# One exp over two PSUM banks in place of two, in the attention phase of a transformer layer on 8 cores

## The reference

```python
x = x + _layernorm(attn(_layernorm(x)))    # x: [4, 4096, 2048]
x = x + _layernorm(ffn(_layernorm(x)))
...
scores = jnp.einsum('bhqd,bhkd->bhqk', q, k) * scale      # 32 half-heads of 64
scores = jnp.where(causal, scores, jnp.finfo(scores.dtype).min)
probs = jax.nn.softmax(scores, axis=-1)
attn_out = jnp.einsum('bhqk,bhkd->bhqd', probs, v)
attn = attn_out[:, 0::2] - lambda_full * attn_out[:, 1::2]
attn = attn * jax.lax.rsqrt(jnp.mean(attn * attn, axis=-1, keepdims=True) + EPS) * ln_w
```

## Time and profile before

| | us |
|---|---|
| median of 3 runs | 10618.79 |
| lowest and highest of them | 10558.02, 11322.63 |
| the profiled execution, its time | 10558.02 |
| its span on the slowest core (core 4) | 10556.5 |
| spans of the 8 cores | 10413.7 to 10556.5 |
| TensorE matmul busy | 8300.7 (79%) |
| ScalarE busy | 3346.5 (32%) |
| VectorE busy | 2612.8 (25%) |

### The profile page before, as it was taken

The page is one execution under the profiler, slowest core; times in us unless marked ns, Lnnn a source line. Parts: engine busy times, 40 slices in busy tenths (PEclk is TensorE's granted clock), DMA queues, the critical chain, the costliest instruction groups (busy, mean ns, idle before and its releaser), DMA issues. The chain is left out here.

```text
span 10556.5 us, 119745 instructions; the slowest of 8 cores (10413.7 to 10556.5 us)
## 1 busy us (share of the span) xinstructions
PE 8300.7 (79%) x43898; PEld 4033.8 (38%) x44754; DVE 2612.8 (25%) x4091; ACT 3346.5 (32%) x4745; POOL 396.6 (4%) x385
## 2 busy tenths in 40 slices
PE   3456456666767774999999999991999999999994
PEld 1233233334434442344444444441344444444442
DVE  2321454433332333111111111115111111111103
ACT  1223455656757773111111112113111111111112
POOL 0000000000000000000000000000000000000000
PEclk8778788888889987999999999995999999998896
DMA  4222301010000003554554554543554554444443
GB/s 105 79 65 72 59 7 39 9 37 4 8 30 10 4 6 97 80 73 67 80 74 66 79 75 66 79 56 127 80 73 67 80 73 66 69 70 75 58 62 80
DMA packets 642913, 635.29 MB, mean 60 GB/s; under 512 B 31247, under 2 KB 619280, under 8 KB 623410
## 3 DMA queue, kind: packets, MB, share of 16 engines
q0 software_dynamic: 569136, 436.44, 28.6%
q1 hardware_dynamic: 73218, 191.14, 5.5%
HBM read 1013.51 MB, written 50.36 MB: 101 GB/s over the span
## 5 line engine op out<-in xcount | busy, mean ns | idle before, releaser
L1248 PE MATMUL p3b_yps<-p3b_hg,p3b_w2c 128*128 128x512 bf16 x12416 | 2846.3, 390 | 167.4 <-DVE p3b_hg L1200 124.2
L1248 PEld LDWEIGHTS p3b_yps<-p3b_hg,p3b_w2c 128*128 128x128 bf16 x12672 | 1253.0, 100 | 1756.5 <-issue 437.8
L617 ACT ACTIVATE p_p<-p_s 128x512 bf16<-128x512 f32 x2816 | 1531.2, 595 | 387.4 <-PE p_s L592 208.1
L1161 PE MATMUL p3b_hps<-p_xfm,p3b_w1A 128*128 128x512 bf16 x6774 | 1526.6, 386 | 52.9 <-DMA p3b_w1A<-rw 45.1
L592 PE MATMUL p_s<-p_q,p_k 128*128 128x512 bf16 x2543 | 969.7, 409 | 668.1 <-ACT p_p L617 416.9
L1161 PE MATMUL p3b_hps<-p_xfm,p3b_w1B 128*128 128x512 bf16 x5642 | 1268.7, 385 | 6.6
L1277 DVE TENSOR_TENSOR p_acc<-p3b_yps,p_acc 128x1024 f32<-128x1024 f32 x544 | 666.2, 1225 | 2434.8 <-PE p3b_yps L1248 2400.4
L1189 ACT ACT_TABLE_LOAD x396 | 508.1, 1283 | 2239.0 <-PE p3b_hps L1161 2221.0
L1161 PEld LDWEIGHTS p3b_hps<-p_xfm,p3b_w1A 128*128 128x128 bf16 x6912 | 681.4, 99 | 896.4 <-issue 172.4
L565 PE MATMUL p_pv<-p_v,p_p 128*128 128x129 bf16 x5632 | 845.6, 230 | 198.7 <-DVE p_p L633 197.4
L633 DVE TENSOR_TENSOR p_p<-p_p,p_mask 128x512 bf16<-128x512 bf16 x1536 | 652.7, 425 | 1395.1 <-ACT p_p L617 1219.7
(11 more groups left out here) (153 smaller groups left out, 3367.2 us busy)
## 6 DMA issues: line engine op xcount, KB each, us to landing
p3b_w2c<-rw POOLq DMA_DIRECT2D x256, 704.0 KB, 7.7
p3b_w1A<-rw POOLq DMA_DIRECT2D x32, 3072.0 KB, 19.2
p3b_w1B<-rw POOLq DMA_DIRECT2D x32, 2560.0 KB, 19.5
p_xt<-xseq SPq DMA_DIRECT2D x32, 1024.0 KB, 12.7
p3a_xm<-xmid_scr SPq DMA_DIRECT2D x32, 1024.0 KB, 8.5
p3b_w2c<-sw POOLq DMA_DIRECT2D x32, 704.0 KB, 7.4
p_xt<-xown SPq DMA_DIRECT2D x16, 1024.0 KB, 11.4
p_xo<-xown SPq DMA_DIRECT2D x16, 1024.0 KB, 6.9
```

Of the source, the lines that this page charges most:

```text
L617: tok = C.inc(eng.activation(out=dst[:], in_=s3_ps[:, bank * 512:(bank + 1) * 512], func=AF.Exp, scale=0.125), "S")
L1161: ins = eng.matmul(out=h_ps[hp][:, ts_ * 512:(ts_ + 1) * 512], lhsT=wbuf[:, dc * width + fcl * 128:dc * width + (fcl + 1) * 128], rhs=xfm2 ...
L1248: ins = eng.matmul(out=y2_ps[cb][:, ts_ * 512:(ts_ + 1) * 512], lhsT=w2c[cw][:, fc * 256 + dcl * 128:fc * 256 + (dcl + 1) * 128], rhs=hg[: ...
```

## The change

The two exps of a slot become one instruction of 1024 elements that reads both banks of `s3_ps`. The four `pbuf` tiles of 512 columns become two of 1024, one for even and one for odd slots, the first map in columns 0 to 511 and the second in 512 to 1023. The counts on ScalarE's semaphore are halved with it. ScalarE waits for the second score matmul of a slot; the first score matmul of slot `s` waits for the whole exp of slot `s - 1`, the second has no wait of its own. In masked slots ScalarE waits for both halves of the mask of slot `s - 2`. VectorE still masks in two instructions of 512, but both come after the whole exp. All matmuls, masks and sizes of the work are otherwise the same.

```diff
-    pbuf = [s2(f"p2_p{i}", [P, 512], BF16) for i in range(4)]
+    pbuf = [s2(f"p2_p{i}", [P, 1024], BF16) for i in range(2)]
...
-                            C.wait(eng, "S", base_S + 2 * s + 2)
-                        p1 = pbuf[s % 2]
-                        p2 = pbuf[2 + s % 2]
+                            C.wait(eng, "S", base_S + s + 1)
+                        pq = pbuf[s % 2]
...
-                                             lhsT=p1[:, tt * 128:(tt + 1) * 128],
+                                             lhsT=pq[:, tt * 128:(tt + 1) * 128],
...
-                                             lhsT=p2[:, tt * 128:(tt + 1) * 128],
+                                             lhsT=pq[:, 512 + tt * 128:512 + (tt + 1) * 128],
...
-                            if k_idx >= 2:
-                                C.wait(eng, "S", base_S + k_idx - 1)
-                            else:
-                                C.wait(eng, "S", sb_prev[bank])
+                            if half == 0:
+                                C.wait(eng, "S", base_S + s if s >= 1 else sb_prev)
...
-                for _k in range(2 * Eg - 2, 2 * Eg):
-                    sbank_last[_k % 2] = base_S + _k + 1
+                sbank_last = base_S + Eg
...
-                        for half in range(2):
-                            k_idx = 2 * s + half
-                            bank = k_idx % 2
-                            C.wait(eng, "T", tok_mm[(s, half)])
-                            if s - 2 >= nm0:
-                                C.wait(eng, "V", base_V + 2 * (s - 2 - nm0) + 1 + half)
-                            dst = (pbuf[s % 2] if half == 0 else pbuf[2 + s % 2])
-                            tok = C.inc(eng.activation(
-                                out=dst[:], in_=s3_ps[:, bank * 512:(bank + 1) * 512],
-                                func=AF.Exp, scale=0.125), "S")
-                            assert tok == base_S + k_idx + 1
+                        C.wait(eng, "T", tok_mm[(s, 1)])
+                        if s - 2 >= nm0:
+                            C.wait(eng, "V", base_V + 2 * (s - 2 - nm0) + 2)
+                        tok = C.inc(eng.activation(
+                            out=pbuf[s % 2][:], in_=s3_ps[:, 0:1024],
+                            func=AF.Exp, scale=0.125), "S")
+                        assert tok == base_S + s + 1
...
-                            C.wait(eng, "S", base_S + 2 * s + 1 + half)
-                            if s - 2 >= 0:
-                                C.wait(eng, "T", tok_pv.get(s - 2, 0))
-                            src = pbuf[s % 2] if half == 0 else pbuf[2 + s % 2]
+                            if half == 0:
+                                C.wait(eng, "S", base_S + s + 1)
+                                if s - 2 >= 0:
+                                    C.wait(eng, "T", tok_pv.get(s - 2, 0))
+                            src = pbuf[s % 2][:, half * 512:(half + 1) * 512]
                             tok = C.inc(eng.tensor_tensor(
-                                out=src[:], in0=src[:],
+                                out=src, in0=src,
```

More of the change, by code:

```diff
@@ L484, in build_program @@
         abf_freeT = [0, 0]
-        sbank_last = [0, 0]
+        sbank_last = 0
         pmask_last = 0
@@ L549, in _ @@
                       nm0=nm0, tok_q=tok_q, base_S=base_S, base_V=base_V,
-                      sb_prev=tuple(sbank_last), pv_cons=pv_cons):
+                      sb_prev=sbank_last, pv_cons=pv_cons):
                     C.wait(eng, f"q1_{tok_q[2]}", tok_q[0])
```

## The result

The change made the kernel slower by 7.4%: the ratio to the kernel before is 1.0742, with a 95% interval of 1.0716 to 1.0768, of 11238 to 11258 us against 10464 and 10477 us. The forecast of 11470 us lay 2% too high, and its range, from 11260, missed the measured time by a few microseconds.

What follows compares the result with a forecast made beforehand. The prediction took the attention phase to be bound by a chain of waits through each PSUM bank, not by one engine. It summed 663 + 31 + 185 = +879 on 10558 to 11437, raised to 11470 us; range 11260 to 11840.

Steps and rivals of the forecast that it cites:

- the clock term: Attention heads start with TensorE at 1.2 GHz and return later: group 0 wholly slow, other heads twice today's time, +185 us.
- the base: Whole kernel before the change: profiled run of 10558 us, raised by half of the 61 us to the median 10618.79.
- unmasked slot at 2.4 GHz: Attention phase: exp 1.02, 0.14 wait, score pair 0.59 and 0.10 wait follow in series, 1.85 us against 1.22 today.
- masked slot at 2.4 GHz: Attention phase: 0.05 us more for VectorE's semaphore, 1.90 against 1.41 today, with mask and PV hidden.
- slot at 1.2 GHz: Attention phase at TensorE's lower clock: the score pair takes 1.06 us, so a slot takes 2.32 us.
- ring and exp, at 2.4 GHz: Attention slots: both banks are freed by one exp and filled for one exp, 2583 us against 1920, +663 us.
- gaps: Between attention heads: the last slot's mask starts after the whole exp and ends 0.49 us later, 64 times, +31 us.
- Rival (a): Attention phase: TensorE's clock returns as early as now, giving 11252 us, or 11310 on the median; chance 16%.
- Rival (b): Attention phase: TensorE stays at 1.2 GHz nearly throughout because each slot has a pause, +1326, 11884 us; chance 14%.
- (c): Masked slots, paced by mask and PV, hide the change; only 640 unmasked steps pay 0.63 each, +403, 10961 us; chance 4%.
- (d): Attention phase: ScalarE's own work sets the pace, so one exp saves 0.18 a slot, -253, 10305 us; chance 3%.
- (e): Attention phase: the score pair is somehow released half-way, loss and saving cancel, no visible change, 10600 us; chance 3%.

Runs made afterwards that it cites:

- the kernel of four narrow banks: The kernel before, with its two 512-wide exps a slot, given four PSUM score banks and packed PV sums: 10357 to 10409 us, against 10446 to 10467 before.

## Why the prediction was right and where it failed

The direction, the mechanism and most prices held; the clock term and the base did not:

| step | forecast | measured |
|---|---|---|
| exp of 1024 | 1.02 us | 1.023 |
| unmasked slot at 2.4 GHz | 1.85 | 1.86 |
| masked slot at 2.4 GHz | 1.90 | 1.91 |
| slot at 1.2 GHz | 2.32 | 2.28 |
| gap between heads | 10.29 | 10.14, 10.2 on average |
| ring and exp, at 2.4 GHz | +663 | +676 |
| gaps | +31 | +24 |
| clock | +185 | +87 |
| sum | +879 | +787 |
| own time of the base | 10558, raised by 33 | 10464, 10477 |
| forecast and result | 11470 | 11238 to 11258 |

The measured +676 is 640 x 1.857 + 704 x 1.907 + 64 x 1.02 = 2596, less 1920; the +87 is 2683 less 2596. The sum agrees with the difference of the two kernels' times, about 777 us. Of the forecast's 223 us too much, 120 are the base, 98 the clock and 7 the gaps, less 13 for the ring; the other 10 are the 787 of the sum against the 777 of the times.

**The clock term** is the step that failed: "I take group 0, masked from its first slot, wholly at 1.2 and in the other 48 heads twice today's time". It was forecast at 185 us and measures 87. Each head starts at 1.2 GHz, as forecast, but group 0 came back like the others (its mean granted clock is 0.78, where below 0.6 was forecast), and all of them after four steps on average, where the kernel before took 3.5. The prediction's own sign of being wrong, "if the clock's mean in the phase stays at 0.86", is what happened. The head's start shows the slow steps of 2.28, each with a ScalarE idle time of 1.25:

```profile
3735.56 1.02 ACT L609 ACTIVATE p_p<-p_s 128x1024 bf16<-128x1024 f32 x1
3737.84 1.02 ACT L609 ACTIVATE p_p<-p_s 128x1024 bf16<-128x1024 f32 x1 [1.25 <-PE p_s L589]
3740.11 1.02 ACT L609 ACTIVATE p_p<-p_s 128x1024 bf16<-128x1024 f32 x1 [1.25 <-PE p_s L589]
3742.39 1.02 ACT L609 ACTIVATE p_p<-p_s 128x1024 bf16<-128x1024 f32 x1 [1.25 <-PE p_s L589]
3744.67 1.02 ACT L609 ACTIVATE p_p<-p_s 128x1024 bf16<-128x1024 f32 x1 [1.25 <-PE p_s L589]
```

The score pair of the second of these steps, on TensorE, after an idle time of 0.40:

```profile
3739.00 1.01 PE L589 MATMUL p_s<-p_q,p_k 128*128 128x512 bf16 x2 [0.40 <-ACT p_p L609]
```

255 of 1344 steps begin at 1.2 GHz, where 392 were assumed (225 did before, on core 0). The return came later in microseconds, 478 us of the heads' slots at 1.2 GHz for 325, but hardly in slots; whether TensorE's pauses within a slot put it off is not shown.

Rival (a), "the clock returns as early as now", describes what happened, and its 11252 us are the measured time, but by luck. It prices the clock at nothing, as if no slot ran at 1.2 GHz, although a return as early as now leaves over 200 such slots, worth the 87 us that it lacks; and its base of 10558 is 88 us too high. The two errors cancel. Rival (b), the one with a page of the Trainium skill beside it, did not occur: the masked slots of groups 1 to 3 are at 1.00, as before, all but one of 528 on core 6.

**The base** is the second error, and a little larger. The sum was made on an execution of 10558 us and raised by 33 for a median of 10619, which makes it 120 us more than the 10464 and 10477. That execution's slowest core, 4, had a mean granted clock of 0.891 where cores 0 to 3 had 0.899 to 0.901. Its attention phase was no longer for it (2866 us, as on cores 0, 1 and 3); the difference lies behind the phase, 6560 us for their 6435 to 6462. Taking the 10440 us of core 3 would have led to 11320, within 1% of the result.

**The gap** grew by 0.34, to 10.14, in most heads (10.2 on average), not by 0.49: two masks with no wait between them start 0.34 apart and take 0.76 us. The 0.91 of the earlier trace rows, from which the 0.49 was read, held the distance of the two exps that they waited for.

Of the other rivals, (c), the masked slots hiding the change, falls with their 1.91; (d), ScalarE as the limit, with the kernel of four narrow banks, in which the same exps run at 0.54 apart in place of 0.61; (e) was never near. The saving by the Trainium skill (ScalarE: Activation LUTs, section What ACT_TABLE_LOAD costs), estimated at 93 ns a slot, measures 60 in the serial ring (1.92 to 1.86) and 50 in the unmasked slots where ScalarE is the limit (0.98 to 0.93).

The slot at 1.2 GHz is 0.04 shorter than forecast: the pair takes 1.01 there and not the 1.06 of the earlier trace rows.

Not settled is how far mask and PV, which lie between two exps in the masked slots of the kernel before, could be shortened; nothing was tried on the gap's own chain of 10 us a head.

## What to carry to other kernels

Merging two instructions that read two buffers also merges the buffers: count how many are left for the producer to fill while the consumer reads, and if that is none, the consumer's time and the producer's add up. Give the wide instruction a second pair of buffers, and look next at the producer's order, which can hold a ring of its own; here that turned a loss of 7.4% into a gain of 3.8%, of which the merge itself is half a per cent. And before building a sum on a profiled run, compare its dies.

## What the hardware showed that was not expected

- TensorE returned to 2.4 GHz after some four slots in both kernels: in the one before its matmuls followed one another in slots of 1.72 us, in the changed one it idled for 0.40 us in slots of 2.28. It then stayed at 2.4 GHz with 0.81 us of idle time in every 1.86.
- A 1024-wide exp that crosses from one PSUM bank into the next pays nothing for it: 1.023 us, 0.81 for 768 columns and 0.60 for 512 lie on one line of 0.83 ns per element.
- Two of the seven executions of the kernel with 20 matmuls in the gap took 26.5 and 33.6 ms, with mean granted clocks of 0.28 to 0.69 on their cores. No other kernel here did that, and why is open.
